# A gated cross-attention layer with routed experts: three changes of order, and the router's operand turned by DMA

## The reference, cut to what matters

```
x = x + tanh(g0) * xattn(layernorm(x), ctx)      # x 4096 x 512, ctx 3202 x 512
x = x + tanh(g1) * moe(layernorm(x))

xattn(hc, hq):  Sim  = hc@w1 + hq@w2 + (hc*w3)@hq.T + b
                A    = softmax(Sim, over hq);  hq_hat = A @ hq
                Batt = softmax(max(Sim, over hq), over rows);  hc_bar = Batt @ hc
                return concat(hc, hq_hat, hc*hq_hat, hc*hc_bar) @ W_qv + b_qv
moe(x):         gates = softmax(x @ w_router + b_router);  top 2 of 8 experts
                each expert takes at most 640 rows, in the order of the rows
                gelu(rows @ w1 + b1) @ w2 + b2, weighted sum over the two
```

## Time and profile before

| | |
|---|---|
| runs | median 2263.67 us of 3 (2260.11 to 2265.87) |
| the profiled execution | 2267.52 us, its span 2265.5 us |
| TensorE busy | 2177.9 us, 96% of the span, granted clock 0.985 on average |
| VectorE, ScalarE, GpSimd busy | 1304.8, 1142.0, 143.4 us |
| chain that ended last | TensorE 89%, VectorE 4%, DMA 3%, ScalarE 1%, issue 1% |
| one maximum (L159), one low part (L202), one high part (L196) | 2.28, 1.28, 1.13 us |

### The profile page before, as it was taken

How to read it: one execution, slowest core, us unless ns; L and a number is a source line. 1 busy time by engine, 2 the same in 40 slices (tenths; PEclk the granted TensorE clock), 3 DMA queues, 4 the chain that set the end, 5 groups by cost and what they waited for, 6 DMA issues and landing times.

```text
span 2265.5 us, 34657 instructions
## 1 busy us (share of the span) xinstructions
PE 2177.9 (96%) x12013; PEld 1125.3 (50%) x12013; DVE 1304.8 (58%) x2667; ACT 1142.0 (50%) x1745; POOL 143.4 (6%) x141
## 2 busy tenths in 40 slices
PE   5999999999999999998999985999999999999997
PEld 3444444444444444443445542646565565646463
DVE  7656566655555665643566676545656564646450
ACT  6655565655556656554433333626354453636260
POOL 0000000000000000000022222010101010110101
PEclk9999999999999999999999997999999999999999
DMA  9534444444444444435888652343433333343411
GB/s 252 124 81 102 109 111 102 107 110 97 93 103 107 111 101 107 102 79 118 233 221 224 200 130 69 118 132 123 108 102 97 106 93 106 93 112 113 131 42 23
DMA packets 484305, 265.86 MB, mean 117 GB/s; under 512 B 423604, under 2 KB 423732, under 8 KB 480172
## 3 DMA queue, kind: packets, MB, share of 16 engines
q1 hardware_dynamic: 471276, 240.70, 40.3%
q0 software_dynamic: 10880, 20.52, 4.6%
q10 hardware_dynamic: 2112, 4.19, 0.6%
HBM read 97.96 MB, written 71.52 MB: 75 GB/s over the span
## 4 chain that ended last, share of the span: by engine, by line
PE 89%; DVE 4%; DMA 3%; ACT 1%; issue 1%; POOL 0%; another core or an unknown queue 0%; SPq 0%; DVEq 0%; POOLq 0%; ACTq 0%
PE ps L1213 22%; PE ps L1229 22%; PE ps L1860 19%; PE ps L1875 18%; PE ps L1610 6%; DMA arena<-arena 1%; DMA rows<-arena 1%; PE ps L363 1%; DMA arena<-in_ctx 1%; DVE arena L735 0%; DVE arena L202 0%; DVE arena L159 0%; PE ps L1620 0%; POOL rows L1419 0%; DMA arena<-rows 0%
## 5 line engine op out<-in xcount | busy, mean ns | idle before, releaser
L1213 PE MATMUL ps<-arena 128*128 128x512 f16 (+1 forms) x2688 | 558.4, 358 | 6.1 <-ACT arena L1031 3.1
L1229 PE MATMUL ps<-arena 128*128 128x512 f16 x2400 | 557.0, 381 | 0.0
L1860 PE MATMUL ps<-arena 128*128 128x320 f16 x3072 | 420.4, 300 | 17.3 <-DMA arena<-rows 17.3
L1875 PE MATMUL ps<-arena 128*128 128x512 f16 x1920 | 415.7, 379 | 0.0
L1213 PEld LDWEIGHTS ps<-arena 128*128 128x128 f16 x2688 | 250.2, 98 | 287.8 <-issue 8.2
L1229 PEld LDWEIGHTS ps<-arena 128*128 128x128 f16 x2400 | 234.9, 98 | 279.0 <-issue 6.0
L1860 PEld LDWEIGHTS ps<-arena 128*128 128x128 f16 x3072 | 301.2, 98 | 136.2 <-issue 17.4
L1031 ACT ACTIVATE arena<-ps,arena 128x512 f32<-128x512 f32 (+1 forms) x224 | 163.6, 731 | 390.6 <-PE ps L1213 390.6
L1875 PEld LDWEIGHTS ps<-arena 128*128 128x128 f16 x1920 | 187.9, 98 | 225.2
L764 DVE SCALAR_TENSOR_TENSOR arena<-arena 128x512 f16<-128x512 f32 x192 | 144.1, 750 | 194.9 <-ACT arena L1052 194.9
L751 DVE TENSOR_REDUCE arena<-arena 128x1 f32<-128x512 f32 (+1 forms) x224 | 139.8, 625 | 193.2 <-ACT arena L1031 192.5
(11 more groups left out here) (229 smaller groups left out, 1370.3 us busy)
## 6 DMA issues: line engine op xcount, KB each, us to landing
arena<-in_L_ffn_w SPq DMA_DIRECT2D x64, 1024.0 KB, 11.4
feats<-arena SPq DMA_DIRECT2D x48, 512.0 KB, 2.8
arena<-in_x SPq DMA_DIRECT2D x32, 512.0 KB, 3.5
rows<-arena SPq DMA_DIRECT2D x13, 774.0 KB, 3.8
out<-arena SPq DMA_DIRECT2D x16, 512.0 KB, 3.0
arena<-in_ctx SPq DMA_DIRECT2D x6, 1024.0 KB, 12.9
arena<-arena SPq DMA_TRANSPOSE x276, 3.0
arena<-in_L_xattn_W_qv ACTq DMA_DIRECT2D x4, 1024.0 KB, 7.6
```

Source lines behind the costliest of these rows:

```text
L1213: mm = pe.matmul(out, qT[:, q, s * KD + k, :], ctxT[:, r * KD + k, a:z], start=(k == 0 and s + r == 0), stop=(k == KD - 1 and s == 1))
L1229: mm = pe.matmul(psO[q], turned, ctxN[:, j, r, :], start=(j + s + r == 0), stop=False)
L1860: mm = pe.matmul(psH[:, f % 2, h, :], w1s[:, s, k * F + f * P:k * F + (f + 1) * P], XT[:, r, k, h * HALF:(h + 1) * HALF], start=(k + s + r ...
L1875: mm = pe.matmul(psO[:, t % 2, :], hT[:, f, s, t * P:(t + 1) * P], w2s[:, r, f * D:(f + 1) * D], start=(f + s + r == 0), stop=(f == KF - 1 ...
```

## The change

1. **Start of attention.** On ScalarE the drains of scores 11, 12 and 13 of the first two units stand ahead of the probabilities that they stood behind: 11 ahead of probability 2, 12 and 13 ahead of probability 3.
2. **Passage.** The four loads of W move from ScalarE's queue to SyncE's, one behind each of the turns 1 to 4 of the last unit's probabilities. The four sums move from behind all probabilities to: one behind each of the probabilities 4, 5 and 6, the last behind them.
3. **Merge, order.** The maxima go one each after blocks 6 to 9, the scales after block 10, and the splits two each after blocks 11 to 14. On TensorE the merge of a row half is written in four parts, and the router stands before the last of them.
4. **Merge, the turn.** `turn_rows` on TensorE and the two copies on ScalarE are gone from the loop. In their place SyncE issues two transposing DMAs per block, from the row buffer to `xT`, behind the store of x1 and ahead of the load of x, and the router waits for them, q by q. The last block keeps the transposes on TensorE.

The diff, cut to its core:

```diff
 # attention, SyncE, last block of turns
                 turn_p(u - 1, c)
+                if last and 1 <= c < 5:
+                    if c == 1:
+                        sp.wait_ge(qk_done, NC * U)
+                    mg.load_weights(sp, c - 1)
...
 # attention, ScalarE, half()
-                if last and not i and c < 4:
-                    if c == 0:
-                        act.wait_ge(qk_done, NC * U)
-                    mg.load_weights(act, c)
                 if last and not i and c == 5:
                     total_weight()
+                if last and not i and c >= 4:
+                    mg.sum_part(act, c - 4)
                 if last and i and c == 0:
-                    for n in range(4):
-                        mg.sum_part(act, n)
+                    mg.sum_part(act, 3)
...
 # attention, ScalarE, start
         scores(FIRST[1][3], 2, 1, 3)
+        scores(FIRST[1][4], 3, 1, 4)
         probabilities(0, 0, 2)
-        scores(FIRST[1][4], 3, 1, 4)
+        scores(FIRST[1][5], 0, 1, 5)
+        scores(FIRST[1][6], 1, 1, 6)
         probabilities(0, 0, 3)
-        scores(FIRST[1][5], 0, 1, 5)
         probabilities(0, 0, 4)
-        scores(FIRST[1][6], 1, 1, 6)
         probabilities(0, 0, 5)
...
 # merge_and_route
-    LAST = 3
-    SPLITS = {2: (0, 1, 2), 3: (3, 4, 5), 4: (6, 7)}
+    LAST = 5
+    SPLITS = {5: (0, 1), 6: (2, 3), 7: (4, 5), 8: (6, 7)}
...
+        def turn_rows(b, v):
+            sp.wait_ge(y_step, YK * (b + 1))
+            apart(sp, sp_passed)
+            for q in range(QT):
+                sp.dma_start_transpose(xT[:, q].rearrange("p s k i -> p (s k) i"), halves[v][:, q, 0:2 * D])\
+                    .then_inc(xt_turned[q], 16)
...
                 store(2 * n + v, v, n)
-                sp.wait_ge(y_step, YK * (2 * n + v + 1))
-                apart(sp, sp_passed)
+                turn_rows(2 * n + v, v)
                 mg.load_x(sp, x, 2 * n + v + 2, v)
...
 # ScalarE, body()
-                for q in range(QT):
-                    act.wait_ge(turned, QT * c + q + 1)
-                    act.copy(xT[:, q].rearrange("p s k i -> p (s k) i"), psR[q]).then_inc(xt_ready, 1)
...
 # TensorE
             for q in range(QT):
+                if last:
+                    pe.wait_ge(xt_ready, q + 1)
+                else:
+                    pe.wait_ge(xt_turned[q], 16 * (c + 1))
...
-            turn_rows(b - 1, 1 - v)
-            merge(b, v, 1, 0, old)
-            router(b - 1)
-            merge(b, v, 1, 1, old)
+            for part in range(4):
+                merge(b, v, 1, part, old)
+                if part == 2:
+                    router(b - 1)
```

More of the change, by code:

```diff
@@ L1363, in merge_and_route @@
         "counted"))
+    xt_turned = [sem(f"xt_turned_{q}") for q in range(QT)]
     sent, row_free = [[sem(f"{name}_{v}") for v in range(2)] for name in ("sent", "row_free")]
@@ L1388, in sync @@
                 store(2 * n + v, v, n)
-                sp.wait_ge(y_step, YK * (2 * n + v + 1))
-                apart(sp, sp_passed)
+                turn_rows(2 * n + v, v)
                 mg.load_x(sp, x, 2 * n + v + 2, v)
-        for v in range(2):
-            store(NB - 2 + v, v, NB // 2 - 1)
+        store(NB - 2, 0, NB // 2 - 1)
+        turn_rows(NB - 2, 0)
+        store(NB - 1, 1, NB // 2 - 1)
     def gpsimd(pool):
@@ L1583, in tail @@
             for q in range(QT):
-                act.wait_ge(turned, QT * c + q + 1)
+                act.wait_ge(turned, q + 1)
                 act.copy(xT[:, q].rearrange("p s k i -> p (s k) i"), psR[q]).then_inc(xt_ready, 1)
@@ L1607, in merge @@
                 pe.wait_ge(y_step, YK * (b - 2) + 2 * q + 2)
-            for k in range(part * FT // 2, (part + 1) * FT // 2):
+            for k in range(part * FT // 4, (part + 1) * FT // 4):
                 for s, r in ((0, 0), (0, 1), (1, 0)):
@@ L1611, in merge @@
                                    start=(k + s + r == 0), stop=(k == FT - 1 and s == 1))
-            if part == 1:
+            if part == 3:
                 mm.then_inc(y_done, 1)
@@ L1622, in turn_rows, with router @@
                 mm.then_inc(turned, 1)
-        def router(c):
-            pe.wait_ge(xt_ready, QT * (c + 1))
+        def router(c, last=False):
             for q in range(QT):
+                if last:
+                    pe.wait_ge(xt_ready, q + 1)
+                else:
+                    pe.wait_ge(xt_turned[q], 16 * (c + 1))
                 for k in range(KD):
@@ L1640, in body @@
             pe.wait_ge(f_loaded[v], 16 * (n + 1))
-            merge(b, v, 0, 0, old)
-            if old:
-                counts(b - 2)
-            merge(b, v, 0, 1, old)
+            for part in range(4):
+                merge(b, v, 0, part, old)
+                if part == 1 and old:
+                    counts(b - 2)
             if not old:
@@ L1658, in tensor @@
         turn_rows(NB - 1, 1)
-        router(NB - 1)
+        router(NB - 1, last=True)
         counts(NB - 1)
```

14 lines of the change are left out of this document (6 added, 8 removed).

## The result

| | median, us | runs |
|---|---|---|
| before | 2263.50 | 4 (2260.11 to 2265.87) |
| changed | 2285.68 | 4 (2282.37 to 2295.58) |

The ratio is 1.0106 [1.0071, 1.0142]: the changed kernel is 22 us slower, where 2256.4 was forecast and 2275 was the end of the range.

What follows compares the result with a forecast made beforehand. TensorE was taken to bound the kernel before, the loop through SyncE's queue the changed merge. Start -2.4, passage -10, merge loop +2.6 and tail +2.5 sum to -7.3, forecasting 2256.4 us against the median; range 2244 to 2275.

Steps and rivals of the forecast that it cites:

- Start, -2.4: Start of attention: earlier drains let the blocked matmuls start sooner, -2.4 us (0 to -2.6), capped by a later drain.
- Passage, -10: Attention to merge: turns 0 and 1 with no load ahead remove TensorE's wait; -10 us (-13.8 to +2).
- one of the signs of being wrong: Passage: turns landing in over 6 us would show the prediction wrong.
- The third rival: Passage gives nothing, each turn waiting for a load or ScalarE for the sums: term -1, in all +2, 2265; chance 0.18.
- The queue of SyncE: Merge: turns issued behind the store, 10.35 and 11.6 us after a block's last merge matmul, the x load 2.6 later.
- the loop through SyncE takes the place of TensorE's own: Merge block: the wait for the turns gives 17.05 us, the same length, so the transposes' 0.9 is not won.
- Landing of a turn, 3.1 us: Merge: the second turn lands 3.1 us after issue, so TensorE waits about 1.1 us before the router.
- Blocks without weight work, 17.3: Merge loop: seven blocks at 17.3 us, 17.05 and a little for added DMA traffic.
- Blocks with weight work, 19.2, the longer ones: Merge loop: seven blocks at 19.2 us, their later scatter running into the feats load.
- Rival 2: Merge: DMA side becomes the bound, blocks near 19.2 throughout, in all +6, 2270; at 20.3 some 2285; chance 0.27.
- The maxima: Merge loop before: 12.7 of its 269.1 us lost in two blocks, one of them with two maxima of 2.28 us.
- Tail, +2.5: Tail after the merge loop: transposes stay on TensorE, VectorE later by 2.1 to 2.7 us, so +2.5.

Runs made afterwards that it cites:

- E1: The kernel before with the changes of order alone (start, passage, maxima and splits), the router's turn left on TensorE and ScalarE: 2241.03 us, ratio 0.9906.
- E4: The changed kernel with twelve matmuls of 128 x 512 into an unused bank added ahead of each router: 2279.49 us, ratio 1.0071.
- E2: The kernel before with only the two turning DMAs per block and the router at three quarters: 2306.70 us, ratio 1.0201.
- E6: The changed kernel with five matmuls of 128 x 512 added ahead of each router: 2273.34 us, ratio 1.0051.
- E7: The changed kernel without the scatter of each row's second expert, two indirect DMAs per block in place of four: 2260.15 us, ratio 0.9988.
- E8: The changed kernel with an unused reduction of 2.28 us added on VectorE at the end of blocks 1 to 5: 2268.89 us, ratio 1.0039.
- E3: The changed kernel, with GpSimd's scatter of each block held until the next block's turns have landed: 2294.16 us, ratio 1.0139.
- E5: The changed kernel with the two turns ahead of the store of x1 in SyncE's queue: 2269.09 us, ratio 1.0028.
- E11: E5 with weight work moved to VectorE's wait for the logits, and expert 0's four 1 MB raw-weight loads spread over blocks 0 to 3: 2237.79 us, ratio 0.9887.

## Why the prediction was wrong, by its steps

**Start, -2.4: right**, in size (-2.45) and in its limit, the drain behind L1062.

**Passage, -10: right in mechanism, -8.4.** Turns 0 and 1 with nothing ahead took away both large waits, and the merge of block 0 starts 10.9 us earlier, 2.45 of it from the start. What was missed is how far the loads stretch the later turns: each was given 3 to 4 us, an estimate that rested on no row, and they landed in 5.3 to 8.2 us, one of the signs of being wrong that the prediction named. The total weight, forecast for 1073.3, came at 1073.0, but 2.45 of that is the start's; the wait of 3.48 is what is left of it. The third rival did not come true. The Trainium skill (DMA: Bandwidth & Descriptors, "Issuing engines are not separate DMA queues") has DMAs run on the same 16 engines whoever issues them. The trace agrees, as the later turns show, but it does not follow that a new order gains nothing. What counted was which transfers stood ahead of the first two turns in time.

**The queue of SyncE: right, but for the first block.** The turns were issued at F + 9.9 in the block shown, the x load 3.6 us behind (2.6 was taken); the counts and the halves were not the limit. The step that followed it is right as well in the form "the loop through SyncE takes the place of TensorE's own". What the prediction did not look at is the first block, where the feats load takes 13.5 us on the queue behind the raw weights already in the kernel before (12.83 now). There nothing waited for what stood behind it; now the turns do. That is 7.7 of the 28.9.

**Landing of a turn, 3.1 us, taken for every block: the failed step.** In the slow block shown the two turns were used 5.5 and 6.2 us after their issue, and TensorE waited 3.4 us where 1.1 was forecast. It was taken from a place where nothing stands beside it. The prediction set the scatter's first issue at T + 12.9, 1.3 us behind the second turn, and looked only for its collision with the feats load. Counted from F it was to come at F + 12.3 and came at F + 9.8, with the turns. Of these 2.5 us, 1.2 are the release: VectorE's first step starts 0.04 us after the router's end (1217.33 + 0.48 to 1217.85), and a gap read in one kernel had been carried over as a constant. In E1, which leaves the turn on TensorE, the gap is 0.04 as well. The other 1.3 are the clock: it moves the block's end back, and route_1 not. From the router's end to F are 3.44 us in the block shown and up to 4.07 in the other long ones, 2.16 where the clock stays up. E4, with the clock at 1.00 and no wait, has the scatter at F + 11.35 (1203.58 - 1192.23), as this says.

**"Blocks without weight work, 17.3": 21.2 to 23.4.** The wait was set at 1.1 and is 3.4; the clock's half speed behind it (1.3 us in this block, 2.1 to 2.7 with all that is neither floor nor wait in the other four) was not in the sum, though the prediction had the earlier trace rows to say that a wait of 3.09 us brings it. Because the loop is closed, both repeat from block to block; E2 shows that this can end without help. E4, E6, E7 and E8 each break it at another place, and most blocks fall to 16.5 to 18.8.

**"Blocks with weight work, 19.2, the longer ones": reversed.** They are the shorter (16.2 to 19.6, one of 22.9). Where the added work of VectorE is a maximum or two splits (2.3 to 2.5 us) the scatter stands 1.5 us or more behind the first turn. The price of the earlier trace rows for a scatter in the feats load is real (E3, E5), but in this order it is paid by slack.

**Rival 2** had the right side and nearly the right size: 19.2 in every block gave 2270, 20.3 gave 2285, and 2285.68 was measured. It named the scatter, x and turns running together. That the number fits so well is in part luck: the mean block is 20.3 only with the first one, 25.0 for another reason, and the others run from 16.2 to 23.4. It was put at 0.27 because "the waits behind the store hardly varied" before, and that was so because nothing behind the store was in the scatter's way but the x load, which has a block of slack. The range left its upper half out.

**The maxima.** The 12.7 us lost before in two blocks were in the prediction's rows, and with one maximum per block all of it came back (E1). In the sum they vanished under the turn's loop. Had the parts been costed one at a time, order -25 and turn -1.5 to +44 (the loop's ends of 254.9 and 300.4 against 256.4), the question would have been put where it belongs.

**Tail, +2.5: +1.4.** The difference is near the 1.2 us of release that was not there; no run tests this.

What stays open: whether contention for the 16 engines or the writing of GpSimd's descriptors stretches turn and scatter. The runs show that together they are slow and apart they are not (E3, E7, E8), not in which part of the path. Nor is the distance at which they stop to matter sharp: in the changed kernel a scatter 0.9 us behind the first turn went with a block of 17.6, one 1.5 us behind with the block of 22.9. Nor is it shown why the clock fell behind two waits of 0.8 us in E3 and not behind 1.05 and 0.78 in the changed kernel.

## What to carry to other kernels

A transfer that moves onto the critical path has to be costed with what is in flight at the moment when it will be issued, not with its landing in a quiet place; write out the issue times of every queue (GpSimd's indirect DMAs among them) around it, and look closely at two that lie within 2 us of each other (in the long blocks of the changed kernel the first scatter DMA and the first turn were 1.5 us or less apart). Where the new wait feeds the loop that sets its own time, reckon with the price repeating from pass to pass, the clock's included; and look for the fix in order, ahead of or behind the neighbour, before giving up the change. Cost the parts of a change that has several one at a time, since here one part hid a gain of 22 us under a loss of 44.

## What the runs showed of the hardware

- Two turns of 256 KB each land in 3.1 us by themselves. Issued together with four indirect DMAs of GpSimd, they were used 5.5 to 6.2 us after issue, and the longest took 6.9. With half of the indirect DMAs one was still used 5.7 us after its issue (E7). With the scatter 1.6 us or more behind the turns none of the ten took over 3.9 (E8, the five early blocks).
- The granted clock fell to half after two waits of 1.93 and 1.49 us with a router half between them, and stayed there for about 2.5 us of work. Waits of 1.05 and 0.78 did not bring it in the changed kernel, nor did a single one of 1.93 in E2; 0.77 and 0.79 did in one block of E3.
- Useless work cost nothing or less than nothing: 2.6 us of matmuls in 14 blocks left the time where it was or below (E4, 2279.5 against 2285.7), and five reductions of 2.28 us on VectorE made the kernel 17 us faster (E8).
- The queue time of a transposing load of 1.5 MB (L249) is itself a measure of what stands beside it: 5.9 us at the least in the changed kernel, 7.5 with the scatter still landing beside it, 11.1 beside a load of 1 MB (E11), 12.8 behind 4 MB.
